# Weight pieces on GpSimd's queue, rounding on GpSimd, the first normalisation's scaling on ScalarE

## The reference, cut to what matters

```
# attention with squared softplus in place of exp, then a layer normalisation
qkv = einsum('btc,fc->btf', x, w_qkv)
scores = einsum('bhqd,bhkd->bhqk', q, k) * 64 ** -0.5
p = softplus(scores); p = p * p; p = p * causal
attn = p / (sum(p, -1) + 1e-9)
x = layernorm(x + einsum('btc,oc->bto', attn @ v, w_proj) + b_proj)
# feed-forward layer with fake-quantised weights and low-rank additions, then a normalisation
scale = max(abs(w)) / 127;  wq = clip(round(w / scale), -128, 127) * scale
h = gelu(x @ Wq_fc.T + b_fc + 2 * (x @ A_fc.T) @ B_fc.T)          # 1024 -> 4096
h = h @ Wq_proj.T + b_proj + 2 * (h @ A_proj.T) @ B_proj.T        # 4096 -> 1024
x = layernorm(x + h)
```

## Time and profile before

| | |
|---|---|
| time, median of 3 runs | 2138.77 us (2138.14 to 2141.71) |
| the profiled execution's own time | 2140.47 us |
| its span, first to last instruction, slowest core | 2138.9 us |
| spans of the eight cores | 2126.6 to 2138.9 us |
| mean granted clock of TensorE, by core | 0.964 to 0.967 |
| busy: PE, DVE, ACT, POOL | 90%, 49%, 40%, 21% of the span |

### The profile page before, as it was taken

One profiled execution on the slowest core, in us unless ns is written; L12 is line 12 of the kernel. 1 busy time (PEld: TensorE's weight loads), 2 busy tenths in 40 slices (PEclk: granted clock), 3 DMA queues, 4 the chain that ended last, 5 costly groups with the idle time before them and its releaser, 6 DMA issues.

```text
span 2138.9 us, 26841 instructions; the slowest of 8 cores (2126.6 to 2138.9 us)
## 1 busy us (share of the span) xinstructions
PE 1929.6 (90%) x8834; PEld 759.0 (35%) x8834; DVE 1042.4 (49%) x1613; ACT 855.0 (40%) x1026; POOL 448.2 (21%) x515
## 2 busy tenths in 40 slices
PE   6897987888987899999867889999999999999998
PEld 2332332222322333322222234444444444444443
DVE  2675887766689777788759731111110101020202
ACT  2464765765422466677533421212222121313130
POOL 1121221221156412222225421111010101010201
PEclk9998998999999999999978999999999999999999
DMA  8656554357466443344485465020202111110101
GB/s 130 149 135 146 155 150 131 100 128 149 122 188 181 131 112 116 114 124 128 125 222 163 133 191 169 30 69 30 70 30 59 40 50 50 50 60 20 60 10 49
DMA packets 118023, 228.35 MB, mean 107 GB/s; under 512 B 59282, under 2 KB 59538, under 8 KB 115186
## 3 DMA queue, kind: packets, MB, share of 16 engines
q1 hardware_dynamic: 109042, 195.03, 30.2%
q0 software_dynamic: 8848, 31.63, 8.7%
HBM read 182.21 MB, written 58.98 MB: 113 GB/s over the span
## 4 chain that ended last, share of the span: by engine, by line
PE 72%; DVE 10%; DMA 8%; issue 6%; POOL 2%; ACT 2%; SPq 0%; DVEq 0%; POOLq 0%; ACTq 0%
PE ps_s L924 20%; PE ps_a L976 10%; PE ps_f L976 10%; PE ps_a L718 8%; PE ps_f L341 8%; PE ps_s L674 6%; PE ps_f L365 5%; DVE a_ph L700 3%; DMA a_bc<-recscr 3%; PE ps_f L616 3%; DVE a_QO L776 2%; DMA recscr<-g_rec 2%; PE ps_f L497 2%; DMA g_den<-a_nd 1%; ACT a_ph L685 1%
## 5 line engine op out<-in xcount | busy, mean ns | idle before, releaser
L685 ACT ACTIVATE a_ph<-ps_s 128x1024 bf16<-128x1024 f32 (+1 forms) x576 | 560.7, 976 | 506.8 <-PE ps_s L674 505.4
L931 ACT ACTIVATE b_h<-ps_s,g_bfc,g_scl 128x512 bf16<-128x512 f32 x256 | 199.1, 778 | 649.1 <-PE ps_s L924 649.1
L924 PE MATMUL ps_s<-b_xT,b_Wfc 128*128 128x512 bf16 x2048 | 444.0, 379 | 0.0
L718 PE MATMUL ps_a<-a_ph,a_V 128*65 128x512 bf16 (+3 forms) x1280 | 354.0, 366 | 94.4 <-DVE a_ph L700 73.5
L700 DVE TENSOR_TENSOR a_ph<-a_ph 128x1024 bf16<-128x1024 bf16 (+1 forms) x576 | 399.9, 719 | 24.9 <-ACT a_ph L685 12.8
L341 PE MATMUL ps_f<-a_xT,a_wqk 128*128 128x512 bf16 x1024 | 307.5, 396 | 35.5 <-DMA a_xT<-xT 16.9
L692 POOL TENSOR_TENSOR a_ph<-a_ph,g_mask 128x256 bf16<-128x256 bf16 x256 | 196.4, 785 | 498.6 <-ACT a_ph L685 497.7
L981 DVE SCALAR_TENSOR_TENSOR g_x<-ps_a,g_scl,g_x 128x512 f32<-128x512 f32 x32 | 24.0, 751 | 566.1 <-PE ps_a L976 566.1
L924 PEld LDWEIGHTS ps_s<-b_xT,b_Wfc 128*128 128x128 bf16 x2048 | 200.4, 98 | 241.6 <-issue 0.2
L674 PE MATMUL ps_s<-a_QO,a_K 64*128 64x512 bf16 (+3 forms) x1280 | 226.3, 367 | 2.6 <-ACT a_QO L351 2.5
L976 PE MATMUL ps_a<-b_Wp,b_h 128*128 128x512 bf16 x1024 | 224.4, 379 | 0.0
(11 more groups left out here) (47 smaller groups left out, 937.1 us busy)
## 6 DMA issues: line engine op xcount, KB each, us to landing
a_w<-wfc SPq DMA_DIRECT2D x64, 512.0 KB, 5.7
a_w<-wpF SPq DMA_DIRECT2D x64, 512.0 KB, 4.5
a_bc<-recscr SPq DMA_DIRECT2D x64, 256.0 KB, 4.4
g_x<-x SPq DMA_DIRECT2D x32, 512.0 KB, 4.0
x1scr<-g_x SPq DMA_DIRECT2D x32, 512.0 KB, 4.0
g_x<-x1scr SPq DMA_DIRECT2D x32, 512.0 KB, 3.2
out<-g_x SPq DMA_DIRECT2D x32, 512.0 KB, 2.6
a_wqk<-wqk POOLq DMA_DIRECT2D x16, 512.0 KB, 7.4
```

The costliest lines, as they stand in the source:

```text
L685: s_read[sl] = P.op("scalar", lambda E: E.activation(dst, src, AF.Softplus, scale=HS ** -0.5), waits=[tok, ph_av[q]])
L718: tok = P.op("tensor", lambda E, c0=c0, n=n, off=off, x0=x0, hd=hd, fin=fin: E.matmul(ps_a[0:65, hd * 512 + c0: hd * 512 + c0 + n], V4[:, ...
L924: tok = P.op("tensor", lambda E, cc=cc, c0=c0: E.matmul(ps, b_Wfc[:, c0:c0 + 128], b_xT[:, (g % 2) * 4096 + cc * 512:(g % 2) * 4096 + (cc ...
L931: h_tok[(g, f)] = P.op("scalar", lambda E: E.activation(b_h[:, f * 512:(f + 1) * 512], ps, AF.Gelu, bias=g_bfc[:, f:f + 1], scale=g_scl[:, ...
```

## The change

Six edits are made together:

1. Every load of a weight piece and every store of a quantised piece is issued by POOL's queue instead of SP's. For the 64 first reads there are six slots instead of three (three of `g_x`, which is idle then). A slot is refilled two ticks after its piece was used.
2. The rounding of a piece runs on POOL.
3. A merge is put right behind the scores of a unit, before the tick's chain matmuls, and only while the front chain has one to six of its matmuls out. Its share of the window is counted anew, window 14 has none of its own, and merges no longer count in the budget of `pump`.
4. For the first normalisation POOL also makes -mean * rstd, one instruction on 128x1, and ACT scales the block by an Identity activation with scale and bias. The second normalisation is unchanged.
5. The first loads come in four pieces: the K half of the first `wqk`, the two halves of the first `xT`, and the Q half; matmul 4 of a K or Q chain waits for the second half of `xT`.
6. The first weight loads no longer wait for the last block of the first `xT`.

```diff
         def load_wqk(gp, after=()):
             pr, sl = gp % NP, gp % 2
-            k_wqk[gp] = P.dma("gpsimd", msem(f"wqk{sl}"), lambda E: E.dma_start(
+            k_wqk[(gp, 0)] = k_wqk[(gp, 1)] = P.dma("gpsimd", msem(f"wqk{sl}"), lambda E: E.dma_start(
                 out=a_wqk[:, sl * 2048:(sl + 1) * 2048], in_=d_wqk[pr, :, :]), waits=after)
+        def load_first():
+            def part(which):
+                k_wqk[(0, which)] = P.dma("gpsimd", msem(f"wqkf{which}"), lambda E: E.dma_start(
+                    out=a_wqk[:, which * 1024:(which + 1) * 1024],
+                    in_=d_wqk[0, :, which * 1024:(which + 1) * 1024]))
+            def rows(c):
+                k_xT[(0, 0, c)] = P.dma("gpsimd", msem(f"xTf{c}"), lambda E: E.dma_start(
+                    out=a_xT[:, c * 2048:(c + 1) * 2048], in_=d_xT[0, 0, :, c * 2048:(c + 1) * 2048]))
+            part(0)
+            rows(0)
+            rows(1)
+            part(1)
...
-        load_wqk(0)
-        load_xT(0, 0)
+        load_first()
...
-                    w = [k_wqk[gp], k_xT[(s, tg)], free] if cc == 0 else ()
+                    w = [k_wqk[(gp, which)], k_xT[(s, tg, 0)], free] if cc == 0 else [k_xT[(s, tg, cc // 4)]]
...
-                    yield 1.0 + merge_some(cc)
+                    yield 1.0
...
+        def w_slot(k):
+            return k % 6 if k < 64 else k % 3
+        def w_tile(k):
+            sl = w_slot(k)
+            return a_w[:, sl * 1024:(sl + 1) * 1024] if sl < 3 else g_x[:, (sl - 2) * 1024:(sl - 1) * 1024]
         def w_load(k):
...
-            w_tok[k] = P.dma("sync", msem(f"w{sl}"), lambda E: E.dma_start(
-                out=a_w[p0:p0 + pn, sl * 1024:(sl + 1) * 1024], in_=src),
-                waits=[w_free[sl], k_xT[(0, 3)]])
+            w_tok[k] = P.dma("gpsimd", msem(f"w{sl}"), lambda E: E.dma_start(
+                out=w_tile(k)[p0:p0 + pn, :], in_=src), waits=[w_free[sl]])
         def w_take(k):
-            for i in range(k, k + 2):
-                w_load(i)
-            after_ticks(2, lambda: w_load(k + 2))
-            return (k % 3) * 1024
+            w_fill(k)
+            after_ticks(2, w_fill)
+            return w_tile(k)
+        def w_fill(upto=None):
+            while w_next[0] < len(w_src) and not w_busy[w_slot(w_next[0])]:
+                if upto is not None and w_next[0] > upto:
+                    return
+                w_load(w_next[0])
+                w_next[0] += 1
+            assert upto is None or w_next[0] > upto
...
-            wz_tok[i] = P.op("vector", lambda E: E.tensor_scalar(
+            wz_tok[i] = P.op("gpsimd", lambda E: E.tensor_scalar(
                 z, z, g_scl[:, 4 + i // 32:5 + i // 32], MAGIC, ALU.mult, ALU.add),
                 waits=[w_tok[k], scl_tok[0]])
...
-                    wb_st[sl] = P.dma("sync", msem(f"wb{sl}"), lambda E: E.dma_start(
+                    wb_st[sl] = P.dma("gpsimd", msem(f"wb{sl}"), lambda E: E.dma_start(
                         out=dst, in_=a_wb[:, sl * 1024:(sl + 1) * 1024]), waits=[tb])
...
-        def merge_some(cc):
-            if cc not in (3, 6):
-                return 0.0
-            mg["seen"] += 1
-            if mg["want"] and mg["took"] * mg["of"] < mg["seen"] * mg["want"]:
+        def merge_some(part):
+            if not chains or mg["took"] >= mg["want"] * part:
+                return
+            c = chains[0]
+            if c.key[0] in ("qk", "v") and 1 <= c.done <= 6:
                 mg["took"] += 1
                 merge_half(mg["done"])
                 mg["done"] += 1
...
+            if n < NT:
+                t = P.op("gpsimd", lambda E: E.tensor_scalar(
+                    g_mv[:, q * 4 + 2:q * 4 + 3], g_mv[:, q * 4:q * 4 + 1], -1.0,
+                    g_mv[:, q * 4 + 3:q * 4 + 4], ALU.mult, ALU.mult), waits=[t])
+            ln_wait[n] = t
...
-            ta = P.op("vector", lambda E: E.tensor_scalar(
-                x, x, g_mv[:, q * 4:q * 4 + 1], g_mv[:, q * 4 + 3:q * 4 + 4],
-                ALU.subtract, ALU.mult), waits=[ln_wait.pop(n)])
+            if n < NT:
+                ta = P.op("scalar", lambda E: E.activation(
+                    x, x, AF.Identity, bias=g_mv[:, q * 4 + 2:q * 4 + 3],
+                    scale=g_mv[:, q * 4 + 3:q * 4 + 4]), waits=[ln_wait.pop(n)])
+            else:
+                ta = P.op("vector", lambda E: E.tensor_scalar(
+                    x, x, g_mv[:, q * 4:q * 4 + 1], g_mv[:, q * 4 + 3:q * 4 + 4],
+                    ALU.subtract, ALU.mult), waits=[ln_wait.pop(n)])
...
-            mg["want"] = {5: 10, 6: 10, 7: 24, 9: 14, 10: 14, 11: 14, 12: 14, 13: 14, 14: 14}.get(gp, 0)
-            mg["took"] = mg["seen"] = 0
+            mg["want"] = {5: 11, 6: 11, 7: 24, 9: 16, 10: 16, 11: 16, 12: 17, 13: 17}.get(gp, 0)
+            mg["want"] += mg["left"]
+            mg["took"] = 0
...
                 emit_scores(u)
+                merge_some(1.0 - (cols_left - u_cols(u)) / cols_all)
             if 2 <= u <= NU + 1:
                 emit_square(u - 2)
             run_due()
             if u < NU:
-                left = sum(c.left for c in chains) + mg["want"] - mg["took"]
+                left = sum(c.left for c in chains)
```

## The result

The changed kernel took 2180.2 us (median of 4 runs, one of them disturbed; 2178.6 without that one). Before, on the same chip, took 2140.2. The ratio is 1.018, with a 95% interval of 1.0156 to 1.0203. It is **slower by 38 us** where 37 us less were forecast. The profiled execution took 2181.8 us, its slowest core spans 2180.2, and the page's busy time of DVE fell from 1042 to 980 us while POOL's rose from 448 to 650.

A forecast was written before the change was run, and what follows sets the result against it. PE was taken to bound attention with merges, DVE the projection stretches. Terms -2 (first loads), -10 (queue, slots), +3 (rounding), -4 (merges), -14 and -10 (scaling) sum to -37 us: 2102 us, range 2074 to 2136.

The forecast's parts named there:

- Reading of before: Whole kernel: feed-forward from 1400 us stays; PE bounds attention with merges at 4.5 matmuls per us, DVE the projection stretches.
- One sign of this part: Projection stretch, 600 to 718 us: DVE's addition, then L622, would no longer be first among PE's waits (26.3 us before).
- slots' alone: Edit 1 if, by the skill's rule, the transfers gain nothing on POOL's queue: -7 us instead of -10.
- a gain of 3: Edit 1: SP's queue, cleared of pieces waiting for a slot ahead of the small transfers, counted as 3 us.
- Rival A: POOL becomes the gate: its in-order work makes masks, then squares, late; 2160 at its middle, 2189 at worst; chance 0.12.
- wrong if: Matmul rate from 736 us falls, squares waiting for masks; or DVE's `a_bc` and `g_den` waits shrink by over a third.
- rival C: Small transfers come free as pieces leave their queue; half of DVE's 75 us of waits goes: 2070 us; chance 0.13.
- the +50 of rounding: Edit 2, rounding on POOL: upper bound of its +3 us term, whose lower bound was -10.

The follow-up runs named there:

- z2: v3 with the tick's square put ahead of the merge's addition in DVE's order: 2114.7 us, ratio 0.9871 to the kernel before.
- base: The kernel before plus six slots, first loads in pieces and ACT's scaling except the last block; loads and stores on SP: 2119.1 us, ratio 0.9885.
- v3: The base plus merges behind the scores, the addition ahead of the tick's square: 2140.2 us, ratio 0.9998 to the kernel before.
- z1: The base with window 14's 14 merges given to windows 5 to 13, inside the chains: 2108.9 us, ratio 0.9837 to the kernel before.
- y1: The kernel before plus ACT's scaling of the first normalisation, except the last block, which DVE scales: 2127.6 us, ratio 0.9923.
- y4: The base plus rounding of the weight pieces on POOL: 2124.1 us, ratio 0.9912 to the kernel before.

## Why the prediction was wrong

**Reading of before: right.** The feed-forward phase, the projection stretches bound by DVE, the windows with merges bound by PE: all bore out. (The 0.219 us per matmul are a little more than the 0.213 that 512 columns take at 2.4 GHz.) So did the start (first scores 1.3 us earlier on the mean of the cores, 2 forecast) and DVE at 76% (below 80%). One sign of this part failed: the addition L666 is still PE's first wait from 600 to 718 us, with the 20.3 us of the list above, 26.3 before.

**Edit 3, forecast -4, measured +24. This is the step that failed most.** The prediction says "the addition now stands before the tick's square in DVE's order and holds it", and prices that at 8 us as the worst. It gives no working for the 8; the one duration in the step is the addition's 0.69 us, and the wait in front of it is put at nothing. That *wait* is the cost: 121.1 us in 88 pieces, up to 5.3 us, with the tick's square behind it. Before, 92.0 us of it stood behind the tick's square, and PE waited for squares in 32 pieces and not in 59. Turning the order round (z2) takes 27 us back. What is then left of edit 3 is 0.9871 against the base's 0.9885, -3 us, which looks like the forecast's -4 but can't be told from nothing. That window 14 gains when its merges leave was right: 15.0 us in v3 and 14.9 in z1 for the 10 us of DVE's work.

**Edit 1, forecast -10, measured +15 (the first loads' -2 included). This is the second step that failed.** Slots and first loads bring 8, of which the start is 1.3, near the "slots' alone" 7. DVE's waits for pieces (19.5 us, 23.2 on the mean of the cores) are 4.0 in the base, and 10.7 once POOL issues the loads. The queue was priced as issue time of POOL that is hidden. It costs 23: the small transfers take longer, the pieces come later, and a load that waits for a slot holds POOL. The prediction counted what leaves SP's queue as a gain of 3 and had no row, and no bound above zero, for what joins the other. The longest wait behind `wo` was called right in length (13.3 us for "about 14") and wrong in place (191 us at `g_den`, not 164 at `recscr`), since POOL's queue had been delayed. The Trainium skill ("DMA: Bandwidth & Descriptors", "Issuing engines are not separate DMA queues") has another issuer save only the time of the issue. The runs agree that the transfers gain nothing, and go beyond it. The Trainium skill ("DMA: Bandwidth & Descriptors", "Queues, rings and completion order") has each DMA engine take turns between queues by the packet. The longer landings fit this, `recscr`'s 4 KB with 2.66 us in the base and 3.30 to 3.58 with the pieces on POOL's queue, but no run here shows the order of the packets.

**Edit 4, forecast -24, measured -16 and then +11.** Alone (y1), window 8 became 9.9 us shorter for 14 and window 14 8.8 for 10, so that the size of the first was too large; in the changed kernel window 8 gained 6.9. The scaling takes 1.24 us on ACT for the 1.02 taken from an activation of the same columns. "ACT's wait holds the next softplus, which has a tick in hand" holds for 31 blocks. The 32nd has gelus behind it. The prediction asked what is queued behind the wait only for the typical one, not for the last.

**Edit 2, forecast +3, measured +6 alone, 10 in z2's order and 21 when undone in the changed kernel.** The durations were right: rounding 1.12 us median (1.3 taken), and full-size squares beside it 1.11 to 1.21 us by core for 0.68, the longest 2.42. All squares of the changed kernel give back some 31 us of DVE's 50 (576 at 0.774 us on the mean, for 0.719 before), but not all to the rounding: added alone (y4) it lengthens them from 0.724 to 0.748 us on the mean of the cores, 14 us. The +3 is within the noise of the +6; that the price would grow to 21 us beside edits 1 and 3 was not in the sum.

**Rival A** had the side, not the mechanism. POOL became a cost, but by its queue; masks hold DVE only 5.4 us longer (10 on the mean of the cores). Of the two signs named as "wrong if", the first came in part: the rate from 736 us fell to 3.8 per us, with PE waiting for squares, though these waited for additions and not for masks. The second did not come. The waits for `a_bc` and `g_den` grew, the other way from rival C: by half on the profiled cores, by a quarter on the mean of all (88 to 111 us). The range's upper end, 2136, left the bounds above zero unused. Even these, +8 for the merges and 0 for the queue, could not reach 2178 without the +50 of rounding, which measured far less. That the time lies between rival A's middle of 2160 and its worst of 2189 is therefore luck.

## What to carry to other kernels

An instruction that waits for another engine's fresh result belongs *behind* the ready ones in its engine's order; its price is its wait, with all that is queued behind it, not its duration. Ask of a moved instruction what stands behind its last occurrence too, above all at a change of phase. Moving large loads to the queue that already carries the big ones is not free because its issue is hidden: here the small transfers of the other queue took longer, and a load that waits for its buffer delayed everything after it on that engine.

## What the runs showed of the hardware

- Squares take longer while POOL adds or rounds: at 853.5 us of the changed kernel a square takes 2.20 us that takes 0.68 alone, while POOL rounds.

```profile
853.52 2.20 DVE L744 TENSOR_TENSOR a_ph<-a_ph 128x1024 bf16<-128x1024 bf16 x1
854.05 1.12 POOL L514 TENSOR_SCALAR a_w<-a_w,g_scl 128x1024 f32<-128x1024 f32 x1
855.97 1.10 PE L762 MATMUL ps_a<-a_ph,a_V 128*65 128x512 bf16 x2 [4.30 <-DVE a_ph L744]
```

The excess, 1.5 us, is more than the 1.12 of the rounding. The issue of a load (853.48 us, 0.53) lies just ahead of it, but issues alone don't lengthen squares: the 131 to 139 full-size ones of each core that overlap an issue and no other work of POOL take at most 0.69 us. The Trainium skill, "SBUF — State Buffer", "Who interferes with whom", has a DVE instruction with two inputs in SBUF and a GpSimd one that reads SBUF lock each other out for a whole instruction; that gives a stop of up to POOL's instruction, and the trace shows somewhat more here.
- An Identity activation of 128x1024 f32 in SBUF takes 1.24 us on ACT, and the two-operation rounding of the same size 1.12 us on POOL and 0.78 on DVE.
- The issues of pieces on POOL's queue take 0.53 to 0.74 us in the changed kernel (192 on each core); only their waits are long.
